# A graph network's attention stages: first units in sections, last units bank by bank, GpSimd divides

## Chip, core and metric

One core of a Trainium2 chip runs the whole program in one launch. The metric is the time of that launch in microseconds (us). The engines are TensorE (PE in the rows; PEld is its weight load), VectorE (DVE), ScalarE (ACT), GpSimd (POOL) and SyncE (SP). A queue that only issues transfers has a q behind its name.

## What is computed

The network has 3125 nodes with 256 features and 100000 edges. Besides norms, small attention blocks, a routed layer of experts and a last dense layer, it has four graph attention layers (`g0` in the first block, `g1`, `g2`, `g3` in the second). Each computes, for a head:

```
h = x @ W
e[s, d] = leaky_relu(al_s[s] + al_d[d], 0.2)        for each edge s -> d
alpha   = exp(e) / sum over the edges into d of exp(e)
out[d]  = sum over the edges into d of alpha * h[s]
```

`g0` has 4 heads of 64 features and a relu; `g1` and `g2` have 4 heads of 128 features and an ELU, y for y > 0 and exp(y) - 1 below; `g3` has one head of 256 features and nothing behind it.

## The kernel before

The attention is dense: a matrix CT of 3125 x 3125 counts holds, for source row and destination column, how many edges there are. `stage_gat_sums` (lines 1616 to 1871) runs once for each layer; its tiles are named `g0a_...` to `g3a_...` in the trace. The nodes are cut into T = 25 tiles of 125 rows. A **unit** is one source tile of one group of heads: NU = 100 units for `g0`, `g1` and `g2` (4 groups of 25) and 50 for `g3` (2 groups of 25). A unit has four steps:

- SP loads the 125 x 3125 counts of the source tile in two parts (lines 67 to 70, called at 1695), into a ring of CR = 3 buffers (`g1`, `g2`) or 4 (`g0`, `g3`, in spare room of the tile HX). From unit CR on it waits for `weighed` of the unit CR before.
- ACT, `rise` (L1794): x = relu(steep * grow - flat), 125 x 3125 elements in one instruction. `grow` holds the factor of each destination, spread over all partitions. From unit 3 on it waits until TensorE has multiplied the unit three before, since x is a ring of 3.
- DVE, `weigh` (L1742): x = (x + flat) * counts, one instruction of 125 x 3125.
- PE (L1866): for each destination tile, a 125 x 125 block of x is the weight and the source tile's features are streamed, 129 columns (122 in `g0`), added up in PSUM over the 25 units of the group. In `g1` to `g3` the destination tiles lie three to a bank in CH = 8 banks, and the columns of the last tile are cut in two and lie in banks 0 and 1; `g0` has CH = 7 banks of four tiles. That is 26 products a unit (25 in `g0`), each run as two passes, so 52 (50) instructions in the rows. Within a unit the banks follow one another; the next unit begins at bank 0 again.

PE waits for all sections of `row_act` before the first product, since the transposes that spread the factors (L1851) use the banks that the products use. ACT copies the spread factors from PSUM into `grow` in three sections of 1125, 1000 and 1000 columns (L1825, `GROUPS`), drains, and only then begins with `rise(0)`.

At the end of a group a bank is moved to `raw` by ACT (L1805, L1807), once the last unit of the group has gone through it (`summed`, `multiplied`). The order on ACT is written out by program order: the 8 moves of the group stand two units behind its last unit, and the `Exp` of the ELU (`lower`, L1814) for bank c stands c + 1 units behind that. So for the last group all eight moves come before the first `Exp`. DVE then does `divide` for each bank: the reciprocal of the sum (L1748), a multiplication (L1757 for `g0`, `g1`, `g2`, L1752 for `g3`), and for the ELU min(y, 0) into `low` (L1760); `elu` (L1769) of a bank, max(exp - 1, y), stands two banks behind `divide`, in the order divide(0), divide(1), elu(0), divide(2), elu(1) and so on. For `g0`, L1763 adds relu(y) into X. For `g1` and `g2` GpSimd issues the write of each finished bank to DRAM, in two parts (lines 69 and 70), out of a ring of YR = 4 buffers, and waits for all of them before the stage can end. In the first three groups these steps lie a unit apart, beside the products of the next group.

```
# the orders on the queues, before
ACT   copy(0) copy(1) copy(2) drain rise(0) rise(1) rise(2) [wait multiplied 1] rise(3) ...
DVE   weigh(0) weigh(1) ...                 last group: divide 0, divide 1, elu 0, divide 2, elu 1, ...
POOL  wait y_ready(n), write(n)             for each bank n of the stage
```

Of the kernel before, what the change touches and what calls it, by code (L numbers as in the profile page):

```python
# [1615 lines left out]
def stage_gat_sums(nc, m, g, AL, HX, OUT, X=None, spare=None, ct_out=()):  # L1616
# [7 lines left out]
    with Stage(nc, g.name + "a") as s:  # L1624
# [57 lines left out]
        @block.sync  # L1682
        def _(sp):
            await_counts(sp, ct_out)
            for n in range(NU):
                if n == CR and S > 1:
                    sp.wait_ge(rows_ready, 1)
                    sp.dma_start(m.RW, turned[:]).then_inc(rows_kept, 16)
                    sp.wait_ge(rows_kept, 16)
                if n >= CR:  # L1690
                    sp.wait_ge(weighed, n - CR + 1)
                h, j = n // T + 1, n % T - CR
                if 0 <= j < 5 and h < S:
# [17 lines left out]
        def _(dve):  # L1711
# [26 lines left out]
            def weigh(n):  # L1738
                dve.wait_ge(risen, n + 1)
                dve.wait_ge(ct_in[n % CR], 32 * (n // CR + 1))  # L1740
                h, sb = head(n), n % T
                nc.vector.scalar_tensor_tensor(out=x[:, n % XR, :], in0=x[:, n % XR, :], scalar=flat[:, h, sb:sb + 1], in1=ct[:, n % CR, :],  # L1742
                                               op0=ALU.add, op1=ALU.mult).then_inc(weighed, 1)

            def divide(gr, c):
# [5 lines left out]
                if g.out == "plain":  # L1751
                    nc.vector.tensor_tensor(OUT[:, t0:t1, gr * F:(gr + 1) * F], raw[:, t0:t1, 0:F], over, ALU.mult).then_inc(divided, 1)  # L1752
                    return
                yt = y[:, n % YR, 0:t1 - t0, :]
                if g.out == "elu" and n >= YR:
                    dve.wait_ge(y_out[n % YR], 32 * (n // YR))
                nc.vector.tensor_tensor(yt, raw[:, t0:t1, 0:F], over, ALU.mult).then_inc(divided, 1)  # L1757
                nc.vector.drain()
                if g.out == "elu":
                    nc.vector.tensor_scalar(low[:, n % 2, 0:t1 - t0, :], yt, 0.0, None, ALU.min).then_inc(low_ready, 1)  # L1760
                else:
                    xt = X[:, t0:t1, gr * F:(gr + 1) * F]
                    nc.vector.scalar_tensor_tensor(out=xt, in0=yt, scalar=0.0, in1=xt, op0=ALU.max, op1=ALU.add)  # L1763
# [22 lines left out]
        @block.scalar  # L1786
        def _(act):
            def rise(n):
# [5 lines left out]
                nc.scalar.activation(x[:, n % XR, :], grow[:, h, :], ACT.Relu, bias=minus[:, h, sb:sb + 1], scale=steep[:, h, sb:sb + 1]).then_inc(risen, 1)  # L1794

# [43 lines left out]
        def _(pe):  # L1839
# [15 lines left out]
            if S > 1:  # L1855
                pe.wait_ge(rows_ready, 1)
            for n in range(NU):
                gr, sb = n // T, n % T
                h0 = gr * (F + 1) - before(gr)
                pe.wait_ge(weighed, n + 1)  # L1860
                for c in range(CH):
                    if sb == 0 and gr * CH + c >= 8:
                        pe.wait_ge(moved, gr * CH + c - 7)
                    bank = bank_of(gr, c)
                    for k, (t, col, f0, f1) in enumerate(pieces(gr, c)):
                        done = nc.tensor.matmul(ps[0:R, bank, col:col + f1 - f0], x[:, n % XR, t * R:(t + 1) * R], whole_row[:, sb, h0 + f0:h0 + f1],  # L1866
                                                start=(sb == 0 and k == 0), stop=(sb == T - 1), skip_group_check=True)
                    if c == CH - 1:
                        done.then_inc(multiplied, 1)
                    elif sb == T - 1:  # L1870
                        done.then_inc(summed, 1)


# [1252 lines left out]
```

## Time and profile before

| What | us |
|---|---|
| median of 3 runs | 3902.7 |
| lowest and highest of them | 3895.01, 3902.9 |
| the profiled execution, its own time | 3902.42 |
| its span, first to last instruction | 3900.3 |
| around the span | 2.1 |
| PE busy in the span | 3489.8 (89%) |
| DVE, ACT, POOL busy | 2067.2, 1702.6, 231.6 |
| mean granted clock of TensorE | 0.933 of full |

The span is that of one execution, and the times of rows are counted from its start. A timeline row gives the start, how long it lasted, the engine, the line, and in brackets how long the engine sat idle before it and what released it; rows with x2 or more hold several instructions back to back.

### The profile page before, as it was taken

The numbers are of one execution on the slowest core, as the hardware profiler recorded it, in microseconds if no ns is written. First come the engines' busy times: TensorE is split into PE (matmuls) and PEld (weight loads), VectorE is DVE, ScalarE is ACT, GpSimd is POOL, SyncE is SP. The second block draws the span as 40 slices with busy tenths as digits, with TensorE's granted clock in tenths as the row PEclk, the third lists the DMA queues.
The fourth block names the chain that finished last, engine by engine and source line by source line (L and its number), as shares of the span: only waits on it lengthen the run. The fifth ranks groups of instructions, "written<-read, shape, count | busy, mean of one in ns | idle before, by whom it ended". The sixth has DMA issues, their size and how long they took to land. (4 is left out here: it accounts for less than half of the span.)

```text
span 3900.3 us, 65697 instructions
## 1 busy us (share of the span) xinstructions
PE 3489.8 (89%) x27372; PEld 3228.9 (83%) x27372; DVE 2067.2 (53%) x2212; ACT 1702.6 (44%) x1945; POOL 231.6 (6%) x320
## 2 busy tenths in 40 slices
PE   3888889999956999878699999788999996899899
PEld 3568879999956999745599999778999996899676
DVE  6665556666653222364367667514667663466421
ACT  0444445555523434232155555414555552455332
POOL 1000000000001222100101001100011001000000
PEclk9879989999967999889799999999999998999979
DMA  3213365655525655501256555324556553654020
GB/s 110 56 33 49 52 139 150 161 159 143 143 78 173 203 188 178 161 15 32 70 150 170 146 163 154 89 80 130 145 163 170 140 153 86 161 138 137 14 56 27
DMA packets 184563, 464.88 MB, mean 119 GB/s; under 512 B 73944, under 2 KB 106465, under 8 KB 182777
## 3 DMA queue, kind: packets, MB, share of 16 engines
q1 hardware_dynamic: 166984, 424.31, 40.0%
q0 software_dynamic: 13904, 33.84, 2.8%
q8 instruction: 209, 3.42, 0.4%
q10 hardware_dynamic: 3399, 2.76, 0.2%
q14 instruction: 67, 0.55, 0.0%
HBM read 407.32 MB, written 53.50 MB: 118 GB/s over the span
## 5 line engine op out<-in xcount | busy, mean ns | idle before, releaser
L1866 PE MATMUL g2a_ps<-HX,g2a_x 125*125 125x129 f32 (+2 forms) x5200 | 574.5, 273 | 7.8 <-DVE g2a_x L1742 7.8
L1866 PE MATMUL g1a_ps<-HX,g1a_x 125*125 125x129 f32 (+2 forms) x5200 | 574.5, 273 | 7.8 <-DVE g1a_x L1742 7.8
L1866 PEld LDWEIGHTS g2a_ps<-HX,g2a_x 125*125 125x125 f32 x5200 | 574.3, 188 | 8.0 <-issue 8.0
L1866 PEld LDWEIGHTS g1a_ps<-HX,g1a_x 125*125 125x125 f32 x5200 | 574.3, 188 | 8.0 <-issue 8.0
L1866 PE MATMUL g0a_ps<-HX,g0a_x 125*125 125x122 f32 x5000 | 548.3, 273 | 7.9 <-DVE g0a_x L1742 7.9
L1866 PEld LDWEIGHTS g0a_ps<-HX,g0a_x 125*125 125x125 f32 x5000 | 548.1, 190 | 8.0 <-issue 8.0
L1742 DVE SCALAR_TENSOR_TENSOR g2a_x<-g2a_x,g2a_flat,g2a_ct 125x3125 f32<-125x3125 f32 x100 | 347.3, 3475 | 188.2 <-ACT g2a_x L1794 188.2
L1742 DVE SCALAR_TENSOR_TENSOR g1a_x<-g1a_x,g1a_flat,g1a_ct 125x3125 f32<-125x3125 f32 x100 | 347.3, 3474 | 188.1 <-ACT g1a_x L1794 188.1
L1742 DVE SCALAR_TENSOR_TENSOR g0a_x<-g0a_x,g0a_flat,HX 125x3125 f32<-125x3125 f32 x100 | 347.3, 3475 | 180.2 <-ACT g0a_x L1794 180.2
L1794 ACT ACTIVATE g2a_x<-g2a_grow,g2a_minus,g2a_steep 125x3125 f32<-125x3125 f32 x100 | 299.3, 2995 | 248.3 <-PE g2a_ps L1866 248.3
L1794 ACT ACTIVATE g1a_x<-g1a_grow,g1a_minus,g1a_steep 125x3125 f32<-125x3125 f32 x100 | 299.3, 2995 | 248.3 <-PE g1a_ps L1866 248.2
L1794 ACT ACTIVATE g0a_x<-g0a_grow,g0a_minus,g0a_steep 125x3125 f32<-125x3125 f32 x100 | 299.1, 2993 | 234.7 <-PE g0a_ps L1866 234.7
L1866 PE MATMUL g3a_ps<-HX,g3a_x 125*125 125x129 f32 (+2 forms) x2600 | 288.6, 273 | 7.9 <-DVE g3a_x L1742 7.9
L1866 PEld LDWEIGHTS g3a_ps<-HX,g3a_x 125*125 125x125 f32 x2600 | 288.5, 189 | 8.0 <-issue 8.0
L2559 ACT ACTIVATE moe_hT<-moe_psh,moe_sm 128x128 f32<-128x128 f32 x448 | 164.2, 367 | 235.0 <-PE moe_psh L2477 208.6
L1742 DVE SCALAR_TENSOR_TENSOR g3a_x<-g3a_x,g3a_flat,HX 125x3125 f32<-125x3125 f32 x50 | 173.6, 3475 | 111.7 <-ACT g3a_x L1794 111.7
L2477 PE MATMUL moe_psh<-moe_xe,moe_wa 128*128 128x128 f32 x1792 | 211.8, 277 | 0.0
L2477 PEld LDWEIGHTS moe_psh<-moe_xe,moe_wa 128*128 128x128 f32 x1792 | 207.2, 194 | 0.1
L1794 ACT ACTIVATE g3a_x<-g3a_grow,g3a_minus,g3a_steep 125x3125 f32<-125x3125 f32 x50 | 149.5, 2993 | 128.7 <-PE g3a_ps L1866 128.6
L2539 DVE TENSOR_SCALAR moe_ys<-moe_psy,WGT 128x256 f32<-128x256 f32 x56 | 27.1, 484 | 319.9 <-PE moe_psy L2488 319.9
L706 ACT ACTIVATE HX<-merge_ps 125x500 bf16<-125x500 f32 (+1 forms) x175 | 93.9, 568 | 195.2 <-PE merge_ps L561 193.1
L2488 PE MATMUL moe_psy<-HX,moe_hT 128*128 x672 | 154.3, 379 | 0.0
(577 smaller groups left out, 3897.0 us busy)
## 6 DMA issues: line engine op xcount, KB each, us to landing
HX<-counted SPq DMA_DIRECT2D x150, 683.6 KB
g1a_ct<-counted SPq DMA_DIRECT2D x100, 683.6 KB
g2a_ct<-counted SPq DMA_DIRECT2D x100, 683.6 KB
moe_wa<-in_L_ffn_W SPq DMA_DIRECT2D x56, 1024.0 KB
counted<-HX SPq DMA_DIRECT2D x12, 1367.2 KB
HX<-counted SPq DMA_DIRECT2D x150, 79.3 KB
g1a_ct<-counted SPq DMA_DIRECT2D x100, 79.3 KB
g2a_ct<-counted SPq DMA_DIRECT2D x100, 79.3 KB
```

Source lines behind the costliest of these rows:

```text
L706: nc.scalar.activation(ct[:, two % 2, :, d0:d0 + n], ps[0:R, job % BANKS, 0:n * T].rearrange("p (d s) -> p s d", s=T), ACT.Copy).then_inc( ...
L1742: nc.vector.scalar_tensor_tensor(out=x[:, n % XR, :], in0=x[:, n % XR, :], scalar=flat[:, h, sb:sb + 1], in1=ct[:, n % CR, :], op0=ALU.add ...
L1794: nc.scalar.activation(x[:, n % XR, :], grow[:, h, :], ACT.Relu, bias=minus[:, h, sb:sb + 1], scale=steep[:, h, sb:sb + 1]).then_inc(risen, 1)
L1866: done = nc.tensor.matmul(ps[0:R, bank, col:col + f1 - f0], x[:, n % XR, t * R:(t + 1) * R], whole_row[:, sb, h0 + f0:h0 + f1], start=(sb ...
L2477: last = nc.tensor.matmul(psh[:, o % 4, 0:ET], wa[:, j % 3, c, o * P:(o + 1) * P], xe[:, j % XE, c, :], start=(c == 0), stop=(c == 1))
L2488: last = nc.tensor.matmul(psy[:, j % 2, 0:D], hT[:, j % 2, c, :], right, start=(c == 0), stop=(c == MH - 1))
L2539: nc.vector.tensor_scalar(ys[:, j % 2, :], psy[:, j % 2, 0:D], WGT[:, j:j + 1], None, ALU.mult).then_inc(y_ready, 1)
L2559: nc.scalar.activation(hT[:, j % 2, o, :], psh[:, o % 4, 0:ET], ACT.Gelu, bias=sm[:, j % IN, 4 + o:5 + o]).then_inc(h_ready, 1)
```

## The change

`parts(n)` gives three sections of 1125, 1000 and 1000 columns for units 0 and 1, and one section for every other unit. `rise` and `weigh` of the first two units issue one instruction for each section, and PE multiplies the destination tiles of a section when that section is weighed; the counting of `risen` and `weighed` follows (`upto`). On ACT each section of `grow` is copied, drained, and unit 0's `rise` of that section follows at once. The last two units of a stage are multiplied together, bank by bank: bank 0 of both, bank 1 of both, and so on. For the ELU, DVE computes `low` = min(raw, 0) * rec straight from `raw`, and GpSimd computes y = raw * rec (`spread_out`), two banks ahead of the write that it issues in the same queue; `elu` on DVE now waits for that multiplication too.

```diff
+        def parts(n):
+            return [(a0, a0 + k) for a0, k, _, _ in GROUPS] if n < 2 else [(0, T)]
+        def upto(n, k=0):
+            return sum(len(parts(i)) for i in range(n)) + k + 1
...
@@ SP
-                    sp.wait_ge(weighed, n - CR + 1)
+                    sp.wait_ge(weighed, upto(n - CR + 1) - 1)
@@ GpSimd
+            def spread_out(n):
+                t0, t1 = tiles[n % CH][0], tiles[n % CH][-1] + 1
+                pool.wait_ge(low_ready, n + 1)
+                if n >= YR:
+                    pool.wait_ge(y_out[n % YR], 32 * (n // YR))
+                nc.gpsimd.tensor_tensor(y[:, n % YR, 0:t1 - t0, :], raw[:, t0:t1, 0:F], rec[:, t0:t1].unsqueeze(2).to_broadcast([R, t1 - t0, F]), ALU.mult).then_inc(divided, 1)
...
-                for n in range(G * CH):
+                for k in range(G * CH + 2):
+                    if k < G * CH:
+                        spread_out(k)
+                    n = k - 2
+                    if n < 0:
+                        continue
...
@@ DVE, weigh
+                for k, (a, b) in enumerate(parts(n)):
+                    dve.wait_ge(risen, upto(n, k))
+                    part = x[:, n % XR, a * R:b * R]
...
@@ DVE, divide
+                if g.out == "elu":
+                    nc.vector.scalar_tensor_tensor(out=low[:, n % 2, 0:t1 - t0, :], in0=raw[:, t0:t1, 0:F], scalar=0.0, in1=over, op0=ALU.min, op1=ALU.mult).then_inc(low_ready, 1)
+                    return
                 yt = y[:, n % YR, 0:t1 - t0, :]
-                if g.out == "elu" and n >= YR:
-                    dve.wait_ge(y_out[n % YR], 32 * (n // YR))
                 nc.vector.tensor_tensor(yt, raw[:, t0:t1, 0:F], over, ALU.mult).then_inc(divided, 1)
                 nc.vector.drain()
-                if g.out == "elu":
-                    nc.vector.tensor_scalar(low[:, n % 2, 0:t1 - t0, :], yt, 0.0, None, ALU.min).then_inc(low_ready, 1)
...
@@ DVE, elu
                 dve.wait_ge(low_exp, n + 1)
+                dve.wait_ge(divided, n + 1)
@@ ACT
                 nc.scalar.activation(row_cols(c), row_bank(c), ACT.Copy).then_inc(row_act, 1)
-            nc.scalar.drain()
-            for n in range(NU + XR + CH):
+                nc.scalar.drain()
+                rise_part(0, *parts(0)[c])
+            for n in range(1, NU + XR + CH):
...
@@ PE
+            for n in range(2):
+                for i, (a, b) in enumerate(parts(n)):
+                    pe.wait_ge(weighed, upto(n, i))
+                    for c in range(CH):
+                        for k, piece in enumerate(pieces(0, c)):
+                            if a <= piece[0] < b:
+                                done = product(n, c, k, *piece)
+                done.then_inc(multiplied, 1)
+            for n in range(2, NU - 2):
...
+            for c in range(CH):
+                for n in (NU - 2, NU - 1):
+                    if c == 0:
+                        pe.wait_ge(weighed, upto(n))
+                    for k, piece in enumerate(pieces(G - 1, c)):
+                        done = product(n, c, k, *piece)
+                if c == CH - 1:
+                    done.then_inc(multiplied, 2)
+                else:
+                    done.then_inc(summed, 1)
```

## Rows read from the trace of the kernel before

**Rows 1.** The page: its first line, and the costliest group of one stage.

```profile
span 3900.3 us, 65697 instructions
...
L1866 PE MATMUL g1a_ps<-HX,g1a_x 125*125 125x129 f32 (+2 forms) x5200 | 574.5, 273 | 7.8 <-DVE g1a_x L1742 7.8
```

**Rows 2.** The timeline at the opening of `g1a`, 1927 to 1950 us.

```profile
1927.85 1.11 ACT L1825 ACTIVATE g1a_grow<-g1a_ps 125x1125 f32<-125x1125 f32 x1 [1.63 <-PE g1a_ps L1851]
1929.53 1.95 ACT L1825 ACTIVATE g1a_grow<-g1a_ps 125x1000 f32<-125x1000 f32 x2 [0.57 <-PE g1a_ps L1851]
1931.57 8.76 ACT L1794 ACTIVATE g1a_x<-g1a_grow,g1a_minus,g1a_steep 125x3125 f32<-125x3125 f32 x3
1934.67 10.24 DVE L1742 SCALAR_TENSOR_TENSOR g1a_x<-g1a_x,g1a_flat,g1a_ct 125x3125 f32<-125x3125 f32 x3 [8.42 <-ACT g1a_x L1794]
...
1938.29 36.92 PE L1866 MATMUL g1a_ps<-HX,g1a_x 125*125 125x129 f32 x312 [7.85 <-DVE g1a_x L1742]
...
1946.66 3.00 ACT L1794 ACTIVATE g1a_x<-g1a_grow,g1a_minus,g1a_steep 125x3125 f32<-125x3125 f32 x1 [6.33 <-PE g1a_ps L1866]
```

**Rows 3.** Stretches: length, busy of PE, PEld, DVE, ACT, POOL (x), granted clock, DMA share, GB/s.

```profile
1925.70:1929.70 4.00, 4.00 (x21) 4.00 (x21) 0.29 (x1) 1.73 (x4) 0.00 (x0) 0.52 1.01 252
1929.90:1932.90 3.00, 0.54 (x5) 0.35 (x4) 0.00 (x0) 2.91 (x3) 0.00 (x0) 1.00 0.47 125
1933.10:1938.20 5.10, 0.00 (x0) 0.00 (x0) 3.53 (x2) 5.10 (x3) 0.00 (x0) 0.50 0.00 0
1938.30:1943.00 4.70, 4.70 (x22) 4.70 (x23) 4.70 (x2) 2.03 (x1) 0.00 (x0) 0.50 0.76 178
...
1946.60:2500.00 553.40, 553.40 (x5035) 553.40 (x5034) 371.36 (x193) 310.06 (x151) 30.97 (x48) 1.00 0.55 152
```

**Rows 4.** The timeline at the end of `g1a`, 2508 to 2536 us.

```profile
2512.78 0.49 ACT L1805 ACTIVATE g1a_raw<-g1a_ps 125x387 f32<-125x387 f32 x1 [0.17 <-PE g1a_ps L1866]
2513.17 0.93 ACT L1814 ACTIVATE g1a_low<-g1a_low 125x384 f32<-125x384 f32 x2
2513.72 0.56 DVE L1769 SCALAR_TENSOR_TENSOR g1a_y<-g1a_low,g1a_y 125x384 f32<-125x384 f32 x1 [2.59 <-ACT g1a_low L1814]
2514.19 0.17 DVE L1748 RECIPROCAL g1a_rec<-g1a_raw 125x3 f32<-125x3 f32 x1
2514.43 0.56 DVE L1757 TENSOR_TENSOR g1a_y<-g1a_raw,g1a_rec 125x384 f32<-125x384 f32 x1
...
2515.83 0.17 DVE L1748 RECIPROCAL g1a_rec<-g1a_raw 125x3 f32<-125x3 f32 x1
...
2525.89 0.73 POOL L69 DMA_DIRECT2D attended<-g1a_y  x1
2526.61 0.57 POOL L70 DMA_DIRECT2D attended<-g1a_y  x1
...
2535.53 0.28 POOL L1190 MEMSET HX<- 125x100 f32 x1 [8.34 <-POOLq L64]
```

**Rows 5.** GpSimd's groups, kept apart by shape: count, busy us, mean ns, idle before.

```profile
L1196 POOL COPY g1p_xs<-XT 128x250 f32 x25 | 9.7, 396 | 37.2 <-PE g1p_ps L1219 37.1
...
L2820 POOL MEMSET ffn_gT<- 5x3125 f32 x1 | 2.7, 2697 | 0.0
```

**Rows 6.** The timeline at the end of `g0a`.

```profile
1097.41 0.51 ACT L1805 ACTIVATE g0a_raw<-g0a_ps 125x260 f32<-125x260 f32 x2 [0.48 <-PE g0a_ps L1866]
...
1098.25 0.17 DVE L1748 RECIPROCAL g0a_rec<-g0a_raw 125x4 f32<-125x4 f32 x1
...
1099.35 0.17 DVE L1748 RECIPROCAL g0a_rec<-g0a_raw 125x4 f32<-125x4 f32 x1
...
1101.01 0.23 DVE L1763 SCALAR_TENSOR_TENSOR X<-g0a_y,X 125x64 f32<-125x64 f32 x1
```

**Rows 7.** The timeline in the second group of `g1a`, one bank's steps beside the products.

```profile
2101.05 2.99 ACT L1794 ACTIVATE g1a_x<-g1a_grow,g1a_minus,g1a_steep 125x3125 f32<-125x3125 f32 x1 [2.31 <-PE g1a_ps L1866]
...
2104.08 3.48 DVE L1742 SCALAR_TENSOR_TENSOR g1a_x<-g1a_x,g1a_flat,g1a_ct 125x3125 f32<-125x3125 f32 x1 [0.59 <-ACT g1a_x L1794]
```

More of the change, by code:

```diff
@@ L1738, in weigh @@
             def weigh(n):
-                dve.wait_ge(risen, n + 1)
                 dve.wait_ge(ct_in[n % CR], 32 * (n // CR + 1))
                 h, sb = head(n), n % T
-                nc.vector.scalar_tensor_tensor(out=x[:, n % XR, :], in0=x[:, n % XR, :], scalar=flat[:, h, sb:sb + 1], in1=ct[:, n % CR, :],
-                                               op0=ALU.add, op1=ALU.mult).then_inc(weighed, 1)
+                for k, (a, b) in enumerate(parts(n)):
+                    dve.wait_ge(risen, upto(n, k))
+                    part = x[:, n % XR, a * R:b * R]
+                    nc.vector.scalar_tensor_tensor(out=part, in0=part, scalar=flat[:, h, sb:sb + 1], in1=ct[:, n % CR, a * R:b * R],
+                                                   op0=ALU.add, op1=ALU.mult).then_inc(weighed, 1)
             def divide(gr, c):
@@ L1753, in divide @@
                     return
+                if g.out == "elu":
+                    nc.vector.scalar_tensor_tensor(out=low[:, n % 2, 0:t1 - t0, :], in0=raw[:, t0:t1, 0:F], scalar=0.0, in1=over, op0=ALU.min, op1=ALU.mult).then_inc(low_ready, 1)
+                    return
                 yt = y[:, n % YR, 0:t1 - t0, :]
-                if g.out == "elu" and n >= YR:
-                    dve.wait_ge(y_out[n % YR], 32 * (n // YR))
                 nc.vector.tensor_tensor(yt, raw[:, t0:t1, 0:F], over, ALU.mult).then_inc(divided, 1)
                 nc.vector.drain()
-                if g.out == "elu":
-                    nc.vector.tensor_scalar(low[:, n % 2, 0:t1 - t0, :], yt, 0.0, None, ALU.min).then_inc(low_ready, 1)
-                else:
-                    xt = X[:, t0:t1, gr * F:(gr + 1) * F]
-                    nc.vector.scalar_tensor_tensor(out=xt, in0=yt, scalar=0.0, in1=xt, op0=ALU.max, op1=ALU.add)
+                xt = X[:, t0:t1, gr * F:(gr + 1) * F]
+                nc.vector.scalar_tensor_tensor(out=xt, in0=yt, scalar=0.0, in1=xt, op0=ALU.max, op1=ALU.add)
             def elu(gr, c):
@@ L1787, in _, with rise_part @@
         def _(act):
+            def rise_part(n, a, b):
+                h, sb = head(n), n % T
+                nc.scalar.activation(x[:, n % XR, a * R:b * R], grow[:, h, a * R:b * R], ACT.Relu, bias=minus[:, h, sb:sb + 1],
+                                     scale=steep[:, h, sb:sb + 1]).then_inc(risen, 1)
             def rise(n):
@@ L1793, in rise @@
                     act.wait_ge(rows_in[h], 80)
-                nc.scalar.activation(x[:, n % XR, :], grow[:, h, :], ACT.Relu, bias=minus[:, h, sb:sb + 1], scale=steep[:, h, sb:sb + 1]).then_inc(risen, 1)
+                for a, b in parts(n):
+                    rise_part(n, a, b)
             def move(gr, c):
@@ L1856, in _, with product @@
                 pe.wait_ge(rows_ready, 1)
-            for n in range(NU):
+            def product(n, c, k, t, col, f0, f1):
                 gr, sb = n // T, n % T
-                h0 = gr * (F + 1) - before(gr)
-                pe.wait_ge(weighed, n + 1)
+                h0, bank = gr * (F + 1) - before(gr), bank_of(gr, c)
+                return nc.tensor.matmul(ps[0:R, bank, col:col + f1 - f0], x[:, n % XR, t * R:(t + 1) * R], whole_row[:, sb, h0 + f0:h0 + f1],
+                                        start=(sb == 0 and k == 0), stop=(sb == T - 1), skip_group_check=True)
+            for n in range(2):
[7 more added lines that the diff above has]
+            for n in range(2, NU - 2):
+                gr, sb = n // T, n % T
+                pe.wait_ge(weighed, upto(n))
                 for c in range(CH):
@@ L1863, in _ @@
                         pe.wait_ge(moved, gr * CH + c - 7)
[L1864 to L1867, printed above, removed]
+                    for k, piece in enumerate(pieces(gr, c)):
+                        done = product(n, c, k, *piece)
                     if c == CH - 1:
@@ L1871, in _ @@
                         done.then_inc(summed, 1)
+            for c in range(CH):
+                for n in (NU - 2, NU - 1):
+                    if c == 0:
+                        pe.wait_ge(weighed, upto(n))
+                    for k, piece in enumerate(pieces(G - 1, c)):
+                        done = product(n, c, k, *piece)
+                if c == CH - 1:
+                    done.then_inc(multiplied, 2)
+                else:
+                    done.then_inc(summed, 1)
 def stage_dense(nc, m, a, ROWS, X, back, mean, rstd):
```

## The prediction

> **What bounds the kernel now.** I read the page first: the span, and the costliest group [rows 1]. Then the stretches of one attention stage with their granted clock [rows 3], and then the timelines at its opening and its end [rows 2, 4]. Inside a stage TensorE is the bound: it worked through the whole of 553.4 us at a granted clock of 1.00, its full 2.4 GHz level [rows 3], and it sat idle before the group only once, 7.8 us ahead of the first product [rows 1]. It ran 5035 passes in that stretch [rows 3], 0.110 us each, so a unit of 52 (5200 passes, 100 units [rows 1]) takes 5.72 us; DVE's 3.48 us and ACT's 2.99 us lie beside it [rows 7]. Nothing in the body can be won by the change. What it can reach is the opening, where TensorE waits for ACT and DVE, and the end, where the other engines work with TensorE done.
>
> In the opening ACT ends its copies at 1929.53 + 1.95 = 1931.48, unit 0 rises until 1934.6, is weighed until 1938.15, and the first product starts at 1938.29 [rows 2]. There TensorE's clock is at its 1.2 GHz level (0.50) for 4.7 to 4.8 us more, having fallen from 1.00 about 2.6 us after the transposes ended at 1930.4 [rows 3]. So unit 0 ends only at 1946.66.
>
> At the end of `g1a` the last bank is moved at 2512.78. Eight banks then go through DVE at 2515.83 - 2514.19 = 1.64 us each, and GpSimd issues its last write until 2527.18; the next stage starts 8.34 us later [rows 4]. GpSimd needs 0.72 + 0.57 = 1.29 us for a bank's two writes [rows 4], and waits for DVE in between.
>
> **Opening, all four stages.** ACT's order becomes copy, drain, section of `rise`, three times. A rise of 3125 columns takes 8.76/3 = 2.92 us back to back [rows 2], an `Exp` of 384 columns 0.465 [rows 4]: that is 0.12 us fixed and 0.90 ns a column, so 1.13 us for 1125 columns and 1.02 for 1000. The drain costs 0.09 (1931.48 to 1931.57) [rows 2]. The copies take 1.11 and 0.975 [rows 2].
> - Copy 0 ends 1928.96, rise 0/0 at 1930.2, copy 1 at 1931.2, rise 0/1 at 1932.3, copy 2 at 1933.3.
> - TensorE still waits for all three copies, so it starts at 1933.3, not 1938.29: **5.0 us earlier**. The sections of rise cannot bring it nearer, since the copies are now behind them.
> - DVE: 3.48 us for 3125 columns and 0.56 for 384 [rows 4, 7] give 1.34 and 1.21 us a section. Section 0 is weighed by 1931.6, section 1 by 1933.5, section 2 by 1935.6. TensorE has 18 passes in section 0 and 16 in section 1, at the lower clock 0.22 us each, so it wants section 1 at 1937 at the earliest. Unit 1 is weighed by 1939.4 and unit 2 by 1944.0, both before unit 0 and unit 1 can be multiplied. No gap.
> - What is added: four more instructions on each of ACT and DVE, some 0.25 us a unit, and two drains; unit 2 rises until 1940.5 against 1940.33 before. They are hidden by TensorE, which is two units behind; without that cover they would cost under 0.5 us a stage.
> - The load of unit 3's counts waits for unit 0 weighed, now 1935.6 and not 1938.15. It is earlier, so is SP's queue behind it.
>
> The other three stages open in the same order with the same widths; I take 5.0 us for each, 20.0 together. How long the clock stays low from the first product is not in the trace for the new order. It was 4.7 us here and 4.0 us for the transposes ahead of it, up to 1929.7 [rows 3]. The lower clock costs half of its stretch. With the shorter idle time ahead I take 3.9 us, a gain of 0.45 us a stage, **1.8 us in all**. The ends of the range: it never falls (2.35 us a stage), or it rises only when it did before.
>
> **Last two units.** TensorE's work is the same, but bank c is complete two products by three times 0.22 = 1.32 us apart and not 0.66, so all banks but the last come earlier. `g0` gains: DVE worked there until 1101.24 while the last move ended 1097.92 [rows 6], 3.3 us behind; a bank costs it 1.1 us, the distance of its reciprocals [rows 6], less than the 1.75 us between banks now (eight products of 0.22), so only one full bank and the small one are left, 1.5 us. Gain **1.8 us**. `g3` has a reciprocal of 0.17 and a multiplication of 0.56 us a bank, as in [rows 4], is hardly behind, and gains the small rest: I put 0.4. `g1` and `g2` gain nothing, because ACT's first `Exp` stands behind all eight moves in its queue, and so DVE's third bank does too. Against it: the last unit is wanted a bank after the unit before it, 4.8 us sooner than before. It is weighed at about that moment; I put 0.3 us for `g0` and 0.1 for each of the others, **0.6 us** lost.
>
> **GpSimd divides (`g1`, `g2`).** DVE loses the multiplication and its drain; its period falls to about 1.2 us. But GpSimd's queue is now: multiplication of bank c + 2, two writes of bank c. Banks 0 and 1 are multiplied while TensorE still works. Bank 2 is ready at 2515.05 (the reciprocal at 2514.19 and 0.86 us more, as in [rows 4]). From then GpSimd has 6 multiplications and 8 times 1.29 = 10.3 us of writes in one queue, and DVE's `elu` of bank c waits for the multiplication behind the write of bank c - 3. So the queue is the bound.
>
> The trace shows no two-input operation on GpSimd. The nearest rows are a copy of 250 columns, 396 ns, and a memset of 3125 columns, 2697 ns or 0.86 ns a column [rows 5]: 0.18 us fixed and 0.33 for 384 columns, 0.51 with one input. That is the lower end. With two inputs read one after the other it is 0.18 + 0.66 = 0.84; I take 0.85, nearest to that row. The upper end, with waits on DVE in it, I put at 2.0, four times the one-input price. Five at 0.85, the wide last bank 1.03, 10.3 of writes, and 0.7 for 14 hand-overs of 0.05: 16.3 us, the last write issued at 2531.35 and not 2527.18. **A loss of 4.2 us a stage, 8.4 in all**; 2.1 a stage at the lower end, 11 at the upper. The 8.34 us behind the last write stay.
>
> The Trainium skill ("GPSIMD Engine Reference", section "Elementwise — side-by-side cycle accounting") speaks against this part: GpSimd needs about 2.6 cycles of 1.2 GHz for an element with two inputs. By it 384 columns are an estimated 0.93 us with dispatch, and the sum would be about 1 us longer. No row here shows it.
>
> In the first three groups the multiplication lies beside TensorE. In the second group unit n rises at 2101.05, when three units before it is done, and is weighed at 2107.56, while TensorE wants it 11.44 us after 2101.05, at 2112.5 [rows 7]: 4.9 us of slack cover one multiplication a unit. Writes of banks 6 and 7 of a group now wait for the next group's first banks, 25 units later; their buffers are not wanted sooner.
>
> **Sum.** -20.0 - 1.8 - 1.8 - 0.4 + 0.6 + 8.4 = -15.0 us on the profiled execution's 3902.4, which lies 0.3 us under the median of the runs: **3887.5 us**. A measurement of this kernel tells about 0.2%, 7.8 us, from no change.
>
> **Rivals.**
> - *The clock does not fall* (0.13). TensorE's idle time ahead of the first product shrinks from 7.85 us to 2.9, and the clock was still at 1.00 2.5 us after the transposes [rows 3]. Against it: it was at 0.50 from 1933.1, before 1933.3. It would give 1.9 us more a stage: 3880.
> - *The clock rises late* (0.05). If it stays low to the moment at which it rose before, the 5.0 us are passed at half speed and 2.5 a stage is left: 3899.
> - *GpSimd and DVE shut each other out* (0.12). Both now read `raw` and `rec` in the same stretch. If each multiplication waits for DVE's `low` and `elu`, 0.56 + 0.55 us [rows 4], the queue is 6.6 us longer a stage: 3900.7, no change. The place decides: DVE can do both while GpSimd issues 1.29 us of writes, which is why I hold it unlikely. The Trainium skill ("SBUF — State Buffer", section "SBUF: two separate sides") says that the two share a port pair, held for a whole instruction against a DVE operation with two SBUF inputs. No row here shows it.
> - *The multiplication is far slower, and the kernel with it* (0.05). GpSimd's queue at the ends of `g1` and `g2` is the place. At 3.0 us each it adds 12.9 us a stage: 3913. It decides from 2.75 us a multiplication, where the loss passes 7.8 us. For it: no two-input row exists. Against it: a memset of eight times the columns takes 2.70 us [rows 5].
>
> My forecast has 0.65. Faster: 0.65 + 0.13 = 0.78; no change: 0.05 + 0.12 = 0.17; slower 0.05. The range goes from the case where the clock stays up with the cheapest multiplications, 3876, to 3897; it leaves out the last three rivals and the far bound.
>
> **What would show it.** In the changed kernel's trace: the first product 5.4 us after the first copy of the factors begins (10.4 now); a rise to clock 1.00 within 3 to 5 us of it; GpSimd's multiplications at 0.5 to 1.0 us; in the ends of `g1` and `g2` GpSimd without idle time from bank 2 on, its last write 18.5 us behind the last move's start (14.4 now), and DVE waiting for it; `g0`'s DVE done about 1.8 us behind the last move. The forecast is wrong if TensorE gets a gap in units 0 to 2, if a multiplication takes over 1.5 us, or if the body's 5.72 us a unit changes.

## The result, and the profile after

The changed kernel took **3889.4 us** (median of 9 runs, 3884.2 to 3894.7) against 3900.1 for the kernel before (9 runs on the same chip): a ratio of 0.9973, with a 95% interval of 0.9963 to 0.9983. That is 10.7 us less, where 15.0 were forecast. The profiled execution of the changed kernel was the slowest of its nine, 3894.65 us. The spans of the two profiled executions differ by 10.2 us.

The page, its first line and two of the groups. The first answers to [rows 1]:

```profile
span 3890.1 us, 65795 instructions
...
L1888 PE MATMUL g1a_ps<-HX,g1a_x 125*125 125x129 f32 (+2 forms) x5200 | 575.3, 273 | 3.2 <-ACT g1a_grow L1852 3.2
...
L1888 PE MATMUL g0a_ps<-HX,g0a_x 125*125 125x122 f32 x5000 | 548.4, 273 | 3.9 <-DVE g0a_x L1764 3.9
```

TensorE's idle time inside `g1a`'s group fell from 7.8 to 3.2 us, and ACT's last copy ends it now. In `g0a` it is DVE that TensorE waits for.

The timeline at the opening of `g1a`, which answers to [rows 2]:

```profile
1921.12 1.11 ACT L1852 ACTIVATE g1a_grow<-g1a_ps 125x1125 f32<-125x1125 f32 x1 [1.63 <-PE g1a_ps L1879]
...
1922.32 1.32 ACT L1811 ACTIVATE g1a_x<-g1a_grow,g1a_minus,g1a_steep 125x1125 f32<-125x1125 f32 x1
1923.55 0.99 ACT L1852 ACTIVATE g1a_grow<-g1a_ps 125x1000 f32<-125x1000 f32 x1
1923.79 1.39 DVE L1764 SCALAR_TENSOR_TENSOR g1a_x<-g1a_x,g1a_flat,g1a_ct 125x1125 f32<-125x1125 f32 x1 [4.27 <-ACT g1a_x L1811]
1924.61 1.22 ACT L1811 ACTIVATE g1a_x<-g1a_grow,g1a_minus,g1a_steep 125x1000 f32<-125x1000 f32 x1
1925.74 0.98 ACT L1852 ACTIVATE g1a_grow<-g1a_ps 125x1000 f32<-125x1000 f32 x1
...
1926.78 9.47 PE L1888 MATMUL g1a_ps<-HX,g1a_x 125*125 125x129 f32 x57 [3.16 <-ACT g1a_grow L1852]
```

The order is the forecast one: copy, section of rise, three times, with DVE's sections between. The first product starts 1926.78 - 1921.12 = 5.66 us behind the first copy (10.44 before, 5.4 forecast). The sections of `rise` take 1.32 and 1.22 us there, where 1.13 and 1.02 had been reckoned.

Stretches of the same stage, with the columns of [rows 3]:

```profile
1922.50:1925.90 3.40, 1.12 (x10) 0.93 (x8) 1.43 (x2) 3.32 (x4) 0.00 (x0) 0.99 0.55 149
1926.20:1926.70 0.50, 0.00 (x0) 0.00 (x0) 0.50 (x1) 0.50 (x1) 0.00 (x0) 0.50 0.03 13
1926.80:1932.60 5.80, 5.80 (x27) 5.80 (x28) 4.84 (x5) 5.79 (x5) 0.00 (x0) 0.50 0.36 88
1933.00:1936.00 3.00, 3.00 (x30) 3.00 (x29) 1.62 (x2) 1.61 (x2) 0.00 (x0) 1.00 0.84 219
```

The clock fell to its 1.2 GHz level less than a microsecond ahead of the first product, and stayed there until about 1932.8, some 6.1 us into the products: longer than before (4.9), not shorter.

The timeline at the end of `g1a`, which answers to [rows 4]:

```profile
2502.19 0.49 ACT L1832 ACTIVATE g1a_raw<-g1a_ps 125x387 f32<-125x387 f32 x1 [0.82 <-PE g1a_ps L1888]
2502.58 0.93 ACT L1841 ACTIVATE g1a_low<-g1a_low 125x384 f32<-125x384 f32 x2
2503.13 0.56 DVE L1790 SCALAR_TENSOR_TENSOR g1a_y<-g1a_low,g1a_y 125x384 f32<-125x384 f32 x1 [7.55 <-ACT g1a_low L1841]
...
2503.85 0.56 DVE L1777 SCALAR_TENSOR_TENSOR g1a_low<-g1a_raw,g1a_rec 125x384 f32<-125x384 f32 x1
...
2506.61 1.54 DVE L1777 SCALAR_TENSOR_TENSOR g1a_low<-g1a_raw,g1a_rec 125x384 f32<-125x384 f32 x1
2506.88 0.84 POOL L1713 TENSOR_TENSOR g1a_y<-g1a_raw,g1a_rec 125x384 f32<-125x384 f32 x1
2507.65 0.75 POOL L69 DMA_DIRECT2D attended<-g1a_y  x1
...
2508.40 0.58 POOL L70 DMA_DIRECT2D attended<-g1a_y  x1
...
2509.00 0.84 POOL L1713 TENSOR_TENSOR g1a_y<-g1a_raw,g1a_rec 125x384 f32<-125x384 f32 x1
...
2519.71 0.57 POOL L70 DMA_DIRECT2D attended<-g1a_y  x1
...
2528.61 0.28 POOL L1190 MEMSET HX<- 125x100 f32 x1 [8.32 <-POOLq L64]
```

GpSimd is the queue that bounds the end, as forecast. It multiplies in 0.84 us, issues two writes in 1.33, and repeats every 2509.00 - 2506.88 = 2.12 us, where DVE's bank took 1.64 before. The last issue ends 18.1 us behind the start of the last move (18.5 forecast, 14.4 before). DVE's `low` takes 0.56 us with GpSimd quiet and 1.54 with a multiplication beside it.

In `g2a` the same end is 0.9 us longer. GpSimd waits there once for a write to land, since the ring of four buffers for y is full, and one of its multiplications takes 1.28 us. The row of that wait:

```profile
3242.37 0.81 POOL L1713 TENSOR_TENSOR g2a_y<-g2a_raw,g2a_rec 125x384 f32<-125x384 f32 x1 [0.56 <-DMA attended<-g2a_y]
```

Put together for each stage (us). "To first product" runs from the first instruction on the stage's tiles. "Products" runs from the start of the first product to the start of the last, and the end from there to the next stage's first instruction (to its first matmul behind `g3`):

| Stage | to first product | products | end | before | after |
|---|---|---|---|---|---|
| `g0` | 17.0 to 13.0 | 548.0 to 549.0 | 5.2 to 3.5 | 570.3 | 565.4 |
| `g1` | 17.2 to 12.5 | 574.2 to 575.1 | 23.1 to 26.7 | 614.5 | 614.3 |
| `g2` | 17.2 to 12.5 | 574.2 to 574.8 | 23.1 to 27.6 | 614.6 | 614.9 |
| `g3` | 17.0 to 11.9 | 288.4 to 289.2 | 3.3 to 2.8 | 308.7 | 303.9 |
| change, all | -18.8 | +3.3 | +6.0 | | -9.5 |

The openings gained, the two ELU stages gave nearly all of it back at their ends, and the products themselves grew a little. Two waits of TensorE are part of that growth. The first stands in `g0`, 46 us into its products, where DVE had waited 2.78 us for counts. The second stands in every stage, behind bank 0 of the last unit but one, where TensorE now wants the last unit and DVE has just weighed it. Their rows, of `g0a` and then of `g1a`:

```profile
585.98 6.86 DVE L1764 SCALAR_TENSOR_TENSOR g0a_x<-g0a_x,g0a_flat,HX 125x3125 f32<-125x3125 f32 x2 [2.78 <-DMA HX<-counted]
...
589.51 1.24 PE L1888 MATMUL g0a_ps<-HX,g0a_x 125*125 125x122 f32 x9 [0.53 <-DVE g0a_x L1764]
```

```profile
2491.33 1.83 PEld L1888 LDWEIGHTS g1a_ps<-HX,g1a_x 125*125 125x125 f32 x16 [0.26 <-DVE g1a_x L1764]
```

### The profile page after: what moved, and what is told of

Same layout as the page of the kernel before. It is cut to its first block and busy times, and to the rows that moved or that the text cites. A ratio compares the mean times of both kernels' runs of the same rounds, so it can differ in the third digit from the quotient of the medians.

```text
span 3890.1 us, 65795 instructions
## 1 busy us (share of the span) xinstructions
PE 3493.5 (90%) x27372; PEld 3230.8 (83%) x27372; DVE 2055.1 (53%) x2164; ACT 1707.1 (44%) x1961; POOL 287.4 (7%) x384
## 5 line engine op out<-in xcount | busy, mean ns | idle before, releaser
L1764 DVE SCALAR_TENSOR_TENSOR g1a_x<-g1a_x,g1a_flat,g1a_ct 125x3125 f32<-125x3125 f32 (+2 forms) x104 | 348.2, 3350 | 194.2 <-ACT g1a_x L1811 185.5
L1764 DVE SCALAR_TENSOR_TENSOR g2a_x<-g2a_x,g2a_flat,g2a_ct 125x3125 f32<-125x3125 f32 (+2 forms) x104 | 348.2, 3350 | 193.5 <-ACT g2a_x L1811 181.8
L1764 DVE SCALAR_TENSOR_TENSOR g0a_x<-g0a_x,g0a_flat,HX 125x3125 f32<-125x3125 f32 (+2 forms) x104 | 347.7, 3349 | 177.0 <-ACT g0a_x L1811 155.6
L1811 ACT ACTIVATE g1a_x<-g1a_grow,g1a_minus,g1a_steep 125x3125 f32<-125x3125 f32 (+2 forms) x104 | 300.6, 2895 | 243.5 <-PE g1a_ps L1888 243.3
L1811 ACT ACTIVATE g2a_x<-g2a_grow,g2a_minus,g2a_steep 125x3125 f32<-125x3125 f32 (+2 forms) x104 | 300.6, 2894 | 243.2 <-PE g2a_ps L1888 243.0
L1811 ACT ACTIVATE g0a_x<-g0a_grow,g0a_minus,g0a_steep 125x3125 f32<-125x3125 f32 (+2 forms) x104 | 300.5, 2893 | 230.4 <-PE g0a_ps L1888 230.2
L1764 DVE SCALAR_TENSOR_TENSOR g3a_x<-g3a_x,g3a_flat,HX 125x3125 f32<-125x3125 f32 (+2 forms) x54 | 174.4, 3234 | 106.5 <-ACT g3a_x L1811 106.4
L1811 ACT ACTIVATE g3a_x<-g3a_grow,g3a_minus,g3a_steep 125x3125 f32<-125x3125 f32 (+2 forms) x54 | 150.8, 2800 | 123.8 <-PE g3a_ps L1888 123.6
```

The costliest lines, as they stand in the source:

```text
L1764: nc.vector.scalar_tensor_tensor(out=part, in0=part, scalar=flat[:, h, sb:sb + 1], in1=ct[:, n % CR, a * R:b * R], op0=ALU.add, op1=ALU.mu ...
L1811: nc.scalar.activation(x[:, n % XR, a * R:b * R], grow[:, h, a * R:b * R], ACT.Relu, bias=minus[:, h, sb:sb + 1], scale=steep[:, h, sb:sb ...
```

## The experiments

Theories to tell apart: (a) the openings bring all of the gain, and GpSimd's division takes more than a third of it back through GpSimd's one queue; (b) the bank-by-bank order gains nothing in `g1` and `g2` because ACT's `Exp` stands behind its eight moves; (c) TensorE's clock after the opening is worth some 2 us a stage, and its idle time is what costs it; (d) the writes on GpSimd's queue are the end's real price. Each ratio is against the kernel before, run on the same chip.

**open_only.** The opening alone: DVE divides as before, and the last two units go one after the other.

```diff
-            for n in range(2, NU - 2):
+            for n in range(2, NU):
...
-            for c in range(CH):
-                for n in (NU - 2, NU - 1):
...
```

> Only the sections of the first two units, on top of the kernel before. Theory (the opening is the whole gain, some of it lost again to TensorE's low clock): the first product comes 12 to 13 us after a stage's start and not 17, the products' span grows by 0.4 to 1 us a stage, so 4 x 4.7 - 3 = 16 us less than before, ratio 0.996. Rival (the three parts hide each other, and the opening alone brings little since the stage's end is set elsewhere): under 8 us less.

Measured: 3880.15 us (5 runs, 3876.67 to 3881.29), ratio 0.9947 (0.9933 to 0.9960), against 3899.69: 19.5 us less. The openings took 13.4, 12.5, 12.2 and 12.3 us to the first product. So this one part is worth nearly twice what the whole change is.

**divide_only.** GpSimd's division alone: one section for every unit, and the last two units one after the other.

```diff
-            return [(a0, a0 + k) for a0, k, _, _ in GROUPS] if n < 2 else [(0, T)]
+            return [(a0, a0 + k) for a0, k, _, _ in GROUPS] if n < 0 else [(0, T)]
...
-            for n in range(2, NU - 2):
+            for n in range(2, NU):
```

> Only GpSimd's multiplication, on top of the kernel before. Theory (GpSimd's queue is the bound at the ends of g1 and g2, 2.13 us a bank against DVE's 1.64): 3.6 to 4.5 us more at each of the two ends, 8 us more in all, ratio 1.002; g0 and g3 do not move. Rival (the loss at these ends comes with the bank-by-bank order, which makes GpSimd start early and in pieces): no change from before.

Measured: 3907.05 us (11 runs, 3902.55 to 3909.94), ratio 1.0019 (1.0010 to 1.0028): 7.4 us more. The two ends are 3.6 and 3.5 us longer (26.7 both), and those of `g0` and `g3` have not moved. Alone this part makes the kernel slower.

**no_divide.** The change without GpSimd's division: DVE multiplies and takes the minimum as before.

```diff
@@ DVE, divide
-                if g.out == "elu":
-                    nc.vector.scalar_tensor_tensor(out=low[:, n % 2, 0:t1 - t0, :], in0=raw[:, t0:t1, 0:F], scalar=0.0, in1=over, op0=ALU.min, op1=ALU.mult).then_inc(low_ready, 1)
-                    return
...
+                if g.out == "elu":
+                    nc.vector.tensor_scalar(low[:, n % 2, 0:t1 - t0, :], yt, 0.0, None, ALU.min).then_inc(low_ready, 1)
```

> The changed kernel with DVE dividing again. Theory (the parts add up): 8 us less than the changed kernel, 18 to 19 us less than before, ratio 0.9952; the ends of g1 and g2 are 23.1 us from the last product to the next stage, as before. Rival (GpSimd's part pays in the body, by freeing DVE): the same as the changed kernel or slower.

Measured: 3879.58 us (5 runs, 3875.82 to 3883.03), ratio 0.9944 (0.9931 to 0.9958). It is 9.8 us below the change. The ends of `g1` and `g2` are 23.0 and 23.2 us, those of before. Open_only is within 0.6 us of it, and the traces say why the bank-by-bank order is worth nothing in sum. It shortens the ends of `g0` and `g3` by 1.5 and 0.4 us. But from the first pass of the last two units to the last pass TensorE needs 11.40 us in `g0` and 11.66 in each of the others, against 10.81 and 11.33 in open_only: 0.59 and three times 0.33, 1.6 us in all.

**warm.** The change, with 22 transposes into an unused bank ahead of TensorE's wait for the last copy. They compute nothing that is used; they only keep TensorE at work.

```diff
+            for j in range(22):
+                nc.tensor.transpose(ps[0:R, 7, 0:R], far[:, 0, j:j + 1].to_broadcast([R, R]), m.ident[0:R, 0:R])
             pe.wait_ge(row_act, NG)
```

> The changed kernel with 22 transposes more on TensorE, into a bank not yet in use, between the spread factors and the first product, so that it isn't idle there. Theory (TensorE's clock falls in the 3.2 us of idle time and the first unit then runs 3.7 to 6 us at the low level): the granted clock stays at 1.00, the products' span shrinks by half of that, 2 to 3 us a stage, 10 us less than the changed kernel in all. Rival (TensorE waits in the sections for DVE, or the chip is slow for another reason): the clock stays up and the span of the products does not shrink, or the fillers delay the first product and nothing is won.

Measured: 3882.66 us (5 runs, 3879.31 to 3885.64), ratio 0.9956 (0.9943 to 0.9970), 6.8 us below the change, less than the 10 expected. The two intervals still overlap a little; the stretches below don't depend on them. The timeline of warm at the opening of `g1a`, and the stretch behind its first product:

```profile
1922.84 2.56 PE L1883 MATMUL g1a_ps<-C,g1a_far 125*125 125x125 f32 x22
...
1926.37 5.87 PE L1890 MATMUL g1a_ps<-HX,g1a_x 125*125 125x129 f32 x51 [0.96 <-ACT g1a_grow L1852]
```

```profile
1926.80:1932.60 5.80, 5.80 (x55) 5.80 (x54) 4.92 (x4) 5.80 (x5) 0.00 (x0) 1.00 0.42 108
```

The idle time ahead of the first product is 0.96 us and the granted clock stays at 1.00: 55 passes in 5.8 us, where the change made 27. In all four stages no product ran at the lower level. The stretches of the products in `g1` to `g3` are 2.7, 2.6 and 2.9 us shorter than in the change, about half of the 6.1, 5.5 and 6.0 us that the change ran at the lower level there. That is theory (c), at a higher price. `g0` gained nothing by it: its products took 0.5 us longer than in the change, since TensorE waited for DVE at four places in its first 50 us, 2.1 us in all, where the change had one wait of 0.5 us.

**exp_order.** The change, with the `Exp` of a bank right behind the next bank's move in ACT's order, in the last group.

```diff
                             move(gr, c)
+                            if g.out == "elu" and gr == G - 1 and c > 0:
+                                lower(gr, c - 1)
+                        if g.out == "elu" and gr == G - 1:
+                            lower(gr, CH - 1)
```

> The changed kernel, but in the last group of g1 and g2 the Exp of a bank stands right behind the next bank's move on ACT, and not behind all eight. Theory (the bank-by-bank order brings nothing to g1 and g2 only because of ACT's program order): DVE and GpSimd work through the banks while TensorE still multiplies; GpSimd's queue of 2.13 us a bank is then the bound from the first bank, its last write is issued 12 us behind the last product and not 18, so 6 us less a stage and 12 us less in all than the changed kernel. Rival (the ends are bound by the writes' landing, 8.3 us behind the last issue): no change.

Measured: 3881.06 us (4 runs, 3876.64 to 3881.78), ratio 0.9951 (0.9935 to 0.9968), 8.3 us below the change. The ends went from 26.7 and 27.6 to 20.6 and 21.4 us, 12.4 together, as expected; by the medians it is less, with intervals that overlap a little. Its timeline at the end of `g1a`:

```profile
2489.81 11.17 PE L1892 MATMUL g1a_ps<-HX,g1a_x 125*125 125x125 f32 x97
...
2493.43 0.53 ACT L1841 ACTIVATE g1a_low<-g1a_low 125x384 f32<-125x384 f32 x1
...
2494.31 0.55 DVE L1790 SCALAR_TENSOR_TENSOR g1a_y<-g1a_low,g1a_y 125x384 f32<-125x384 f32 x1
...
2499.15 0.56 DVE L1777 SCALAR_TENSOR_TENSOR g1a_low<-g1a_raw,g1a_rec 125x384 f32<-125x384 f32 x1
2499.38 1.01 POOL L1713 TENSOR_TENSOR g1a_y<-g1a_raw,g1a_rec 125x384 f32<-125x384 f32 x1
```

The first bank's `elu` runs at 2494.31, with TensorE at work until 2500.98. In the change the `elu` of bank 0 had to wait until all eight banks were moved (2503.13, behind the last move of 2502.19). Theory (b) holds. Whether the new place of the `Exp` would bring as much without the bank-by-bank order was not run.

**low_one_input.** The change, with DVE's `low` as three or four instructions that read one tensor each and take `rec` as a scalar for each partition.

```diff
-                    nc.vector.scalar_tensor_tensor(out=low[:, n % 2, 0:t1 - t0, :], in0=raw[:, t0:t1, 0:F], scalar=0.0, in1=over, op0=ALU.min, op1=ALU.mult).then_inc(low_ready, 1)
+                    for t in range(t0, t1):
+                        done = nc.vector.tensor_scalar(low[:, n % 2, t - t0, :], raw[:, t, 0:F], rec[:, t:t + 1], 0.0, ALU.mult, ALU.min)
```

> The changed kernel, but DVE computes low tile by tile, raw times a factor that is a scalar of the partition, then the minimum: three or four instructions with one tensor input in place of one with two. Theory (GpSimd's multiplication and a DVE operation shut each other out only when the latter reads two tensors): the low of a bank is no longer stretched to 1.5 us while GpSimd multiplies; its instructions take 0.2 to 0.3 us each, as alone. Rival (any DVE operation on these tiles waits for GpSimd): one of the three takes about 0.8 us more. In both cases the end of the stage does not move by more than 0.5 us, since GpSimd's queue is the bound.

Measured: 3888.24 us, against 3900.39. That is one run, so it gives no verdict on the time; the trace answers the question. Its timeline at the end of `g1a`:

```profile
2502.95 0.68 DVE L1778 TENSOR_SCALAR g1a_low<-g1a_raw,g1a_rec 125x128 f32<-125x128 f32 x3
...
2505.89 1.76 DVE L1778 TENSOR_SCALAR g1a_low<-g1a_raw,g1a_rec 125x128 f32<-125x128 f32 x3
2506.10 0.84 POOL L1713 TENSOR_TENSOR g1a_y<-g1a_raw,g1a_rec 125x384 f32<-125x384 f32 x1
```

The three take 0.68 us alone and 1.76 with the multiplication beside them. Giving up the second tensor input does not free DVE from GpSimd, and the ends are 26.8 us both, close to the change's 26.7 and 27.6.

**rows_first.** The change, with the write of the factor rows issued ahead of the loads of the later units' counts.

```diff
-                if n == CR and S > 1:
+                if n == 1 and S > 1:
```

> The changed kernel, but SP writes the factors' rows behind the first load of counts and not behind all three or four. Theory (in g0 the counts' loads now come too late, the fifth of them because SP waits for a write that is queued behind four loads): DVE's wait for loads in g0, 21.3 us, falls by 5 us or more and the products' span of g0 by 0.5 to 1 us; g1 to g3 don't move; total 1 us less, inside what can be told. Rival (the loads themselves are the limit in g0's opening, at 240 GB/s): the waits stay.

Measured: 3891.59 us (10 runs, 3886.77 to 3898.11), ratio 0.9979 (0.9970 to 0.9989): no gain. In its profiled execution DVE's waits for loads in `g0` did fall as expected, from 21.3 to 16.3 us, and the wait of 0.53 us behind them is gone. But the three versions below that keep this order have waits of 22.2 to 22.9 us again, so the order has not been shown to be the cause. `g0a` needs 13.8 us to its first product. What delays it is seen in the change's own timeline at the opening of `g0a`:

```profile
536.11 0.32 SPq L69 DMA_DIRECT2D HX<-counted  x1
...
538.07 1.33 ACT L1811 ACTIVATE g0a_x<-g0a_grow,g0a_minus,g0a_steep 125x1125 f32<-125x1125 f32 x1
...
541.74 7.37 DVE L1764 SCALAR_TENSOR_TENSOR g0a_x<-g0a_x,g0a_flat,HX 125x1125 f32<-125x1125 f32 x6 [6.47 <-DMA HX<-counted]
...
543.27 8.97 PE L1888 MATMUL g0a_ps<-HX,g0a_x 125*125 125x122 f32 x65 [3.08 <-DVE g0a_x L1764]
```

Unit 0's first section has risen at 539.4, but DVE waits until 541.74 for its counts, 5.6 us behind the issue of their load at 536.11. The order of the queue behind that load is not what delays it; the load starts too late for the earlier rise. In the code SyncE's queue begins the stage with a wait until the counts, which an earlier stage writes, have landed (`await_counts`). With the same opening, `g0` took between 12.9 and 14.9 us to its first product in the ten versions with sections.

**best.** no_divide with the orders of exp_order, warm and rows_first together.

```diff
@@ SP
-                if n == CR and S > 1:
+                if n == 1 and S > 1:
...
@@ DVE, divide
+                if g.out == "elu":
+                    nc.vector.tensor_scalar(low[:, n % 2, 0:t1 - t0, :], yt, 0.0, None, ALU.min).then_inc(low_ready, 1)
...
@@ ACT
+                            if g.out == "elu" and gr == G - 1 and c > 0:
+                                lower(gr, c - 1)
...
@@ PE
+            for j in range(22):
```

> All that the runs so far point to: the sections, the bank-by-bank order, DVE dividing again, the fillers on TensorE, the Exp behind the next bank's move, the factors' rows written early. Theory: 3879.6 of the version in which DVE divides, less 7 for the clock, less 16 for the ends of g1 and g2 (DVE's 1.64 us a bank begins 9 us before the last product and the last write is issued 6 us behind it and not 14.4), less 1: 3856 us, ratio 0.989. Rival (the ends are bound by something behind the last write, or the fillers cost elsewhere): 3870 or more.

Measured: 3863.43 us (4 runs, 3860.82 to 3864.95), ratio 0.9904 (0.9888 to 0.9921). The median is 7 us above the 3856 expected. The ends are 15.8 and 16.8 us, so 13.6 us shorter and not 16. `g0` needed 14.8 us to its first product, and its product stretch still had 3.4 us at the lower level; the other three had none.

**best_sp.** best, with the ELU's writes issued by SyncE's queue, between its loads of counts. The wait for their landing moves to that queue with them.

```diff
-                    pool.wait_ge(y_ready, n + 1)
-                    tile_dma(pool, OUT[...], y[...], y_out[n % YR])
+                sp.wait_ge(y_ready, q + 1)
+                tile_dma(sp, OUT[...], y[...], y_out[q % YR])
```

> The version best, but the finished banks of g1 and g2 are written to DRAM from SP's queue and not from GpSimd's. Theory (most of the 8.3 us between the last write's issue and the next stage is spent by GpSimd's queue, since the last bytes move 1.5 us behind the issue): the next stage starts 3 to 4 us behind the last issue, 4 to 5 us less a stage, 9 us less in all than best, 3854 us. Rival (it is the landing in DRAM, whichever queue issues): 8 us stay, and the time is that of best.

Measured: 3844.48 us (4 runs, 3841.57 to 3850.95), ratio 0.9860 (0.9843 to 0.9876), where 3854 had been expected. Its timeline at the end of `g1a`:

```profile
2501.18 0.55 DVE L1790 SCALAR_TENSOR_TENSOR g1a_y<-g1a_low,g1a_y 125x384 f32<-125x384 f32 x1
...
2502.83 0.55 DVE L1790 SCALAR_TENSOR_TENSOR g1a_y<-g1a_low,g1a_y 125x384 f32<-125x384 f32 x1
...
2506.70 0.47 SPq L70 DMA_DIRECT2D attended<-g1a_y  x1
2509.99 0.28 POOL L1190 MEMSET HX<- 125x100 f32 x1 [594.77 <-POOLq L64]
```

From the end of the last issue to the next stage it takes 2509.99 - 2507.17 = 2.8 us, where it was 8.3 with GpSimd's queue. Where the 8.3 go is read from stretches behind the last write, first of the change and then of best_sp (the last two columns are the DMA share and GB/s):

```profile
2520.30:2521.00 0.70, 0.00 (x0) 0.00 (x0) 0.00 (x0) 0.00 (x0) 0.00 (x0) 0.50 1.07 252
2521.00:2522.00 1.00, 0.00 (x0) 0.00 (x0) 0.00 (x0) 0.00 (x0) 0.00 (x0) 0.50 0.25 76
2522.00:2528.50 6.50, 0.00 (x0) 0.00 (x0) 0.00 (x0) 0.00 (x0) 0.00 (x0) 0.50 0.00 0
```

```profile
2507.70:2508.70 1.00, 0.00 (x0) 0.00 (x0) 0.00 (x0) 0.00 (x0) 0.00 (x0) 0.50 0.61 152
2508.70:2509.90 1.20, 0.00 (x0) 0.00 (x0) 0.00 (x0) 0.00 (x0) 0.00 (x0) 0.50 0.00 0
```

In the change the bytes have moved by 2522 and then no byte moves and no compute instruction runs for 6.5 us; with SyncE's queue that dead time is 1.2 us. The ends are 9.4 and 9.8 us, 13.4 us shorter than in best. Since issue and wait moved together, the run does not tell which of the two costs the time on GpSimd's queue.

**divide_sp.** best_sp with GpSimd's division back.

```diff
@@ the lines of GpSimd, against the changed kernel
-                for k in range(G * CH + 2):
+                for k in range(G * CH):
                     if k < G * CH:
                         spread_out(k)
-                    n = k - 2
...
```

> The version best_sp, but with GpSimd multiplying again, as in the changed kernel; its queue now holds nothing but the multiplications. Theory (GpSimd's part loses only because it shares its queue with the writes): the multiplication of 0.84 us hides beside DVE, DVE's period falls below the 1.32 us between banks, and the ends of g1 and g2 are 1.5 to 2.5 us shorter than in best_sp (9.4 and 9.8 us from the last product to the next stage): 3 to 5 us less in all, ratio 0.985. Rival (GpSimd and DVE keep each other waiting, low is stretched from 0.56 to 1.5 us as in the changed kernel's end): the period is 2 us a bank and the ends are 2 to 5 us longer than in best_sp.

Measured: 3845.22 us (4 runs, 3843.73 to 3847.17), ratio 0.9865 (0.9848 to 0.9881), the same as best_sp, where 3 to 5 us less had been expected. Its timeline at the end of `g1a`:

```profile
2490.28 1.08 POOL L1730 TENSOR_TENSOR g1a_y<-g1a_raw,g1a_rec 125x384 f32<-125x384 f32 x1 [0.49 <-DVE g1a_low L1785]
...
2490.84 0.94 DVE L1785 SCALAR_TENSOR_TENSOR g1a_low<-g1a_raw,g1a_rec 125x384 f32<-125x384 f32 x1
...
2491.86 1.08 POOL L1730 TENSOR_TENSOR g1a_y<-g1a_raw,g1a_rec 125x384 f32<-125x384 f32 x1 [0.49 <-DVE g1a_low L1785]
```

With the writes gone from its queue GpSimd has time left (0.49 us idle a bank), yet a bank still takes 1.58 us, against 1.65 in best_sp: `low` is 0.94 us and not 0.56, the multiplication 1.08 and not 0.84. What DVE hands over it loses again in its longer `low`. The ends are 9.1 and 9.6 us, against 9.4 and 9.8.

## Why the prediction was right, point by point

- **Verdict and range.** Faster by 0.27%, inside the range. The forecast was 1.9 us too low, but that closeness is in part luck. It stood on 3902.4 us for the kernel before, which then measured 3900.1. The forecast of the difference, -15.0 us, misses the medians' -10.7 by 4.3 us. The stage table gives -9.5, and its terms follow.
- **Openings, -20.0.** Measured -18.8: `g1` to `g3` gained 4.8, 4.8 and 5.2, as worked out from the orders on ACT and DVE. `g0` gained 4.1, because of the load of its first counts. The working looked only at whether later loads came earlier.
- **The clock, -1.8.** This term failed. It was taken as low for 3.9 us from the first product. In the profiled execution it was 3.4, 6.1, 5.5 and 6.0 us in `g0` to `g3`, against 4.7, 4.9, 4.9 and 5.0 before: 1.5 us more in sum, so a loss of 0.7 us and not a gain of 1.8. A shorter pause did not give a shorter low stretch. In open_only, with the same opening, it was 4.9, 5.8, 3.4 and 3.2 us, so the term varies by more than 1 us of time from stage to stage and from version to version. The profiled execution was also the slowest, with a mean granted clock of 0.934 where the other eight had 0.935 to 0.938; in the median one the loss may have been less. The rival "the clock does not fall" did not come about in the change. Warm brought it about, and it was worth 2.6 to 2.9 us a stage in `g1` to `g3`, where the rival had 1.9, since the change's low stretches were longer than the forecast's.
- **Last two units, -1.8 and -0.4, +0.6.** `g0` gained 1.7 and `g3` 0.4 at their ends, as forecast, and `g1` and `g2` nothing, for the reason given; exp_order shows it. The late weighing was put at 0.6 us and costs 1.6: 0.59 in `g0` and 0.33 in each of the others. TensorE's idle time there is only 0.33 and 0.07 us; its passes also follow one another later around the wait. So this part gained 0.6 us, and not 1.6.
- **GpSimd divides, +8.4.** +3.7 and +4.5 at the two ends, 8.2 together, and +7.4 by divide_only. The multiplication was taken at 0.85 us from a copy's row with its columns read twice; it is 0.84. The Trainium skill's rate ("GPSIMD Engine Reference", section "Elementwise — side-by-side cycle accounting") gave an estimated 0.93; the trace is nearer to the other sum. The work of a bank was put at 0.85 and 1.29 us; it is 0.84 and 1.33, and it repeats every 2.12. Not foreseen was GpSimd's wait of 0.56 us for a write in `g2`.
- **A wait that the sum did not have.** In the body of `g0` TensorE lost 1.0 us around its wait of 0.53 us for DVE, which had waited for counts. The forecast saw only that units 0 to 2 have no gap, and they have none.
- **What is left.** -18.8 + 0.7 + 1.6 + 1.0 + 6.0 = -9.5, which is the stage table. The product stretches' 3.3 us are its middle three terms. Against the spans' -10.2, 0.7 us lie outside the four stages.
- **The rival in which GpSimd and DVE shut each other out.** Its mechanism is there and its price is not. DVE's `low` is stretched from 0.56 to 1.54 us, but the 1.33 us of writes behind each multiplication let DVE catch up, and in the full queue of `g1` the multiplication keeps its 0.84. Where the writes are gone (divide_sp), it takes away the worth of the division. The Trainium skill ("SBUF — State Buffer", section "SBUF: two separate sides") has the two share a port pair; a GpSimd operation, or a DVE operation with two SBUF inputs, holds it for the whole instruction while the other is blocked. The stretched times agree with that. The Trainium skill also gives the pair to whichever starts first. That agrees in exp_order, where `low` starts 0.23 us ahead, keeps its 0.56, and the multiplication takes 1.01. It does not fit the change, where `low` started 0.27 us ahead and was the one stretched; by which rule it was decided there stays open. The Trainium skill names operations in a two-port mode there beside those with two inputs. A `TENSOR_SCALAR` was stretched as well (low_one_input); whether it ran in such a mode no row tells.
- **The signs.** Of what should show it, the first product (5.66 us), GpSimd's last write (18.1) and `g0`'s DVE (1.6 behind the last move) came as written. The rise of the clock within 3 to 5 us came only in `g0`.

## What to carry to other kernels

When an engine is given work "because it is idle", add up its whole queue at the place where the stage ends: here 0.84 us of multiplication behind 1.33 us of issuing writes made GpSimd the slowest of three, and cost 7.4 us (divide_only) of the 19.5 that the opening won. A part that is cut finer gains only as far as the next engine's program order lets it; moving each `Exp` ahead of the later moves shortened the two ends by 12.4 us, the bank-by-bank order alone by nothing. An order that wants its last input sooner has a price too: here 1.6 us against 2.2 gained. At a stage's end look at the time between the last byte and the next instruction: changing the queue that issues the writes took the ratio from 0.9904 to 0.9860, more than the whole change did. The two ends account for 13.4 us of it.

## What the runs showed of the hardware that was not expected

- A stage whose last writes go through GpSimd's queue waits 8.3 us behind the last issue, of which 6.5 show no byte and no instruction. With SyncE's queue it is 2.8 and 1.2 us in `g1` (3.2 us in `g2`). Where the 6.5 us go the traces do not say.
- In the versions with sections and without fillers TensorE paused for 2.3 to 3.4 us ahead of the first product of `g1` to `g3`, and then ran products at the 1.2 GHz level for 3.1 to 6.3 us. The length of the pause did not decide it: of three pauses of 2.3 us, all in `g1`, two were followed by 3.4 us at the lower level, beginning 1.5 us into the products (no_divide, low_one_input), and one by none (rows_first). With the pause filled but for 0.6 to 1.0 us, the granted clock stayed at 1.00 in all four stages of warm.
- A two-input multiplication of 384 columns takes GpSimd 0.81 to 0.86 us, one of 512 columns 1.03 to 1.06. Some took 1.01 to 1.29 us, and 1.29 for 512 columns; at the places looked at in the ends a DVE instruction with two inputs was under way as each of these began (1.06 and 1.28 us in `g2` of the change, 1.08 and 1.29 in divide_sp).
